# First attention of a two-layer block: block-diagonal queries with full-height score products, and maxima six slots ahead

## The chip, the cores and the metric

The kernel runs on one core of a Trainium2 chip. Its metric is device time in microseconds; the median of three runs before the change is 1698.66 us. The engines named below are TensorE (PE for products, PEld for its weight loads), VectorE (DVE), ScalarE (ACT), GpSimd (POOL) and SyncE (SP), which issues the transfers.

## What is computed

Two layers, each an attention and a feed-forward network with a mixture of experts, over x of 32 batch elements, 128 tokens, 128 features. The change touches the first attention alone, whose 16 heads have 8 features each:

```python
def _L0_xattn_ref(q, k, v, Wq, bq, Wk, bk, Wv, bv, Wo, bo):
    qh = (q @ Wq.T + bq).reshape(B, S, H, Hd).transpose(0, 2, 1, 3)
    kh = (k @ Wk.T + bk).reshape(B, S, H, Hd).transpose(0, 2, 1, 3)
    vh = (v @ Wv.T + bv).reshape(B, S, H, Hd).transpose(0, 2, 1, 3)
    scores = jnp.einsum('bhqd,bhkd->bhqk', qh, kh) / jnp.sqrt(jnp.float32(Hd))
    attn = jax.nn.softmax(scores, axis=-1)
    out = jnp.einsum('bhqk,bhkd->bhqd', attn, vh)
    return out.transpose(0, 2, 1, 3).reshape(B, S, D) @ Wo.T + bo

x = x + _L0_xattn_ref(_layernorm(x), ctx_1024, ctx_1024, ...)   # then ffn 0, attention 1, ffn 1
```

## The kernel before, in words

Blocks follow one another: loads, a small block that rounds a constant `sel0`, the weights of layer 0 (`layer0_weights`), the first attention (`attention0`), its feed-forward network, the second attention, the second network. Each is a block with a barrier at its end, so only `attention0` and what stands ahead of it are touched.

`attention0` works in slots. Slot s is half of the heads of batch element b = s // 2, so there are 64 slots; a group is 4 batch elements, 8 slots. Each engine has one list of instructions, written slot by slot, and waits on semaphores.

- In a slot PE computes the scores of slot s (`scores`), the product of probabilities and values of slot s - 2 (`values`, 24 small products), and the maxima products of slot s + `LM0` (`maxima`). On even slots it also transposes the row maxima (`transpose_maxima`) and projects (`project`); on odd slots it transposes the attention output (`transpose_att`).
- In five of a group's eight slots there is one `fill` as well: transposed x (kind 0), transposed context (1), queries (2), keys (3), values (4) of a later group. All fills and `transpose_maxima` share one PSUM bank, `F_BANK`; each is emptied by ACT (upper half) and DVE (lower half, `lower`) before the next may write it.
- A head's 8 features, split in a high and a low fp16 part, become a contraction of 32 rows (4 combinations of high and low). Queries and keys are written to DRAM (`spill`) and read back four times (`q_x`, `k_x`), so that head 4r + i stands in rows 32i to 32i + 31 of slice r. Products use 32 of the array's 128 rows; two that stand in different row groups are issued side by side. The negated row maxima are added to the scores by a second product with the constant `sel0`.
- ACT takes the exponential of 1024 columns twice per slot (f32 `probs`, fp16 `p_hi`); POOL forms `p_lo` from them; DVE takes the row maxima.
- `transpose_maxima` waits until the last fill has been lowered; `values` of a batch element's first half waits for `s_x`, the residual add (`add`) of the one before, as they share the bank `PV`.

Of the kernel before, what the change touches and what calls it, by code (L numbers as in the profile page):

```python
# [16 lines left out]
P = 128  # L17
# [565 lines left out]
LM0 = 4  # L583
RING0 = 4


def fill_of(s):

    g, at = divmod(s + 11, 8)
    if at < 5 and 0 <= g < G:  # L590
        return g, at
    return None


def fills_before(s):
    return sum(1 for t in range(-11, s) if fill_of(t))


def attention0(nc, mem, psum, x_all, ctx_all, const, w, dram):

    NP = 2 * B
    FIRST, LAST = -11, NP + 4
# [3 lines left out]
    def sb(name, shape, dt=F32):  # L606
        return mem.enter_context(nc.sbuf_tensor(f"{name}_a0", shape, dt))
# [4 lines left out]
    ident, sel = const["ident"], const["sel0"]  # L612
# [6 lines left out]
    q_x, k_x = sb("q_x", [P, 2, 4, 512], F16), sb("k_x", [P, 2, 4, 512], F16)  # L619
    v_hi, v_lo = sb("v_hi", [P, 2, GB, H, D0 + 1], F16), sb("v_lo", [P, 2, GB, H, D0 + 1], F16)  # L620
    negmax, negmax_t = sb("negmax", [P, 2, P]), sb("negmax_t", [P, 2, P], F16)
# [3 lines left out]

    T_BANK, M_BANK, PV, F_BANK = psum[:, 0:4, :], psum[:, 4:6, :], psum[:, 6, :], psum[:, 7, :]
# [4 lines left out]
    s_spill, s_spread = sem("spill"), sem("spread")  # L631
# [4 lines left out]
    with nc.Block() as block:  # L636

        @block.sync
        def _(sp):
            for g in range(G):  # L640
                for m, (hl, wide) in enumerate(((q_hl, q_x), (k_hl, k_x))):
                    sp.wait_ge(s_lo, 5 * g + 3 + m)
                    if g:
                        sp.wait_ge(s_spread, 128 * g)
                    sp.dma_start(dram[m, g % 2], hl[:, :, :]).then_inc(s_spill, 16)
                    sp.wait_ge(s_spill, 32 * g + 16 * m + 16)
                    if g >= 2:
                        sp.wait_ge(s_sc, 8 * (g - 2) + 8)
                    for t in range(4):
                        part = t // 2 if m == 0 else t % 2  # L650
                        src = dram[m, g % 2].rearrange("(r p) l n -> l p r n", p=32)[part]
                        sp.dma_start(wide[t::4, g % 2, :, :], src).then_inc(s_spread, 16)

        @block.tensor
        def _(pe):
            def scores(s):
                b, j = divmod(s, 2)
                tok = slice(b % GB * P, (b % GB + 1) * P)
                par = b // GB % 2
                pe.wait_ge(s_nmt, b + 1)  # L660
                if s >= 2:
                    pe.wait_ge(s_exp_hi, s - 1)
                for r in range(4):
                    for i in (2 * j, 2 * j + 1):
                        rows = slice(32 * i, 32 * i + 32)
                        o = T_BANK[:, 2 * (s % 2) + i % 2, r * P:(r + 1) * P]
                        nc.tensor.matmul(o, k_x[rows, par, r, tok], q_x[rows, par, r, tok], start=True, stop=False)
                    for i in (2 * j, 2 * j + 1):
                        rows = slice(32 * i, 32 * i + 32)
                        o = T_BANK[:, 2 * (s % 2) + i % 2, r * P:(r + 1) * P]  # L670
                        last_ = nc.tensor.matmul(o, sel[rows, r, :], negmax_t[rows, b % 2, :], start=False, stop=True)  # L671
                last_.then_inc(s_sc, 1)

            def maxima(s):
                b, j = divmod(s, 2)
                tok = slice(b % GB * P, (b % GB + 1) * P)
                par = b // GB % 2
                if s % 8 == 0:
                    pe.wait_ge(s_spread, 128 * (s // 8) + 128)
                if s >= 1:  # L680
                    pe.wait_ge(s_max, s)
                for r in range(4):
                    for i in (2 * j, 2 * j + 1):
                        rows = slice(32 * i, 32 * i + 32)
                        last_ = nc.tensor.matmul(M_BANK[:, i % 2, r * P:(r + 1) * P], q_x[rows, par, r, tok],  # L685
                                                 k_x[rows, par, r, tok], start=True, stop=True)
                last_.then_inc(s_mm, 1)

            def transpose_maxima(b, s):
                pe.wait_ge(s_max, 2 * b + 2)  # L690
                if n := fills_before(s):
                    pe.wait_ge(s_lo, n)
                nc.tensor.transpose(F_BANK[:, 0:P], negmax[:, b % 2, :], ident[:]).then_inc(s_nmt_mm, 1)

            def values(s):
                b, j = divmod(s, 2)
                par = b // GB % 2
# [5 lines left out]
                for r in range(4):  # L703
                    for i in (2 * j, 2 * j + 1):
                        h = 4 * r + i
                        o = PV[:, h * (D0 + 1):(h + 1) * (D0 + 1)]
                        q = slice((4 * (i % 2) + r) * P, (4 * (i % 2) + r + 1) * P)
# [64 lines left out]
        def _(act):  # L772
            def fill(s):
# [5 lines left out]
                elif kind < 4:  # L779
                    if g:  # L780
                        act.wait_ge(s_spill, 32 * (g - 1) + 16 * (kind - 1))
                    m = kind - 2
                    nc.scalar.activation((q_hl, k_hl)[m][:, 0, :], F_BANK, ACT.Identity,
                                         bias=w["bias"][:, m:m + 1]).then_inc(s_hi, 1)
                else:
                    if g >= 2:
                        act.wait_ge(s_pv, 8 * (g - 2) + 8)
                    nc.scalar.activation(v_hi[:, g % 2, :, :, 0:D0].rearrange("p j h d -> p (j h) d"),
                                         F_BANK.rearrange("p (h d) -> p h d", d=D0), ACT.Copy).then_inc(s_hi, 1)

            act.wait_ge(s_set, 1)
            for s in range(FIRST, LAST):
# [16 lines left out]
                if even and 0 <= s + LM0 - 2 < NP:  # L809
                    b = (s + LM0 - 2) // 2  # L810
                    act.wait_ge(s_nmt_mm, b + 1)
                    if b >= 2:
                        act.wait_ge(s_sc, 2 * b - 2)
                    nc.scalar.activation(negmax_t[:, b % 2, :], F_BANK[:, 0:P], ACT.Copy, bias=lifted).then_inc(s_nmt, 1)
# [4 lines left out]
        def _(dve):  # L819
# [11 lines left out]
            def lower(s):  # L831
# [11 lines left out]
                else:  # L843
                    last_ = nc.vector.tensor_tensor(
                        v_lo[:, g % 2, :, :, 0:D0].rearrange("p j h d -> p (j h) d"),
                        F_BANK.rearrange("p (h d) -> p h d", d=D0),
                        v_hi[:, g % 2, :, :, 0:D0].rearrange("p j h d -> p (j h) d"), ALU.subtract)
                last_.then_inc(s_lo, 1)

            def maxima(s):  # L850
                b, j = divmod(s, 2)
                dve.wait_ge(s_mm, s + 1)
                if j == 0 and b >= 2:
                    dve.wait_ge(s_nmt_mm, b - 1)
                out = negmax[:, b % 2, 64 * j:64 * j + 64].rearrange("p (i n) -> p i n", n=32)[:, :, 0:4]
                nc.vector.tensor_reduce(out, M_BANK.rearrange("p i (r k) -> p i r k", k=P), AX.X, ALU.max,  # L856
                                        negate=True).then_inc(s_max, 1)
# [17 lines left out]
            nc.vector.memset(negmax[:, :, :], 0.0)  # L875
# [4 lines left out]
            for s in range(FIRST, LAST):  # L880
# [9 lines left out]
                if s % 8 == 2 and (s + 14) // 8 < G:  # L890
                    statistics((s + 14) // 8)

        @block.gpsimd
        def _(pool):
# [14 lines left out]

            normal(0)  # L910
            for s in range(FIRST, LAST):
                if s % 8 == 3 and (s + 13) // 8 < G:
                    normal((s + 13) // 8)
# [448 lines left out]
def program(nc, a, out, spill):  # L1362

    with ExitStack() as mem:
# [18 lines left out]
        def rounded(name, shape, dram, scope):  # L1383

            t = scope.enter_context(nc.sbuf_tensor(name, shape, F16))
            raw_ = scope.enter_context(nc.sbuf_tensor(name + "_raw", shape, F32))
            s1, s2 = (scope.enter_context(nc.semaphore(f"{name}_{i}")) for i in range(2))
            with nc.Block() as block:

                @block.sync  # L1390
                def _(sp):
                    sp.dma_start(raw_[:], dram).then_inc(s1, 16)

                @block.scalar
                def _(act):
                    act.wait_ge(s1, 16)
                    nc.scalar.activation(t[:], raw_[:], ACT.Copy)
            return t

# [29 lines left out]
        with ExitStack() as scope:  # L1429
# [3 lines left out]
            const["sel0"] = rounded("sel0", [P, 4, P], a["c_sel0"], scope)  # L1433
# [86 lines left out]
def constants():  # L1520
# [4 lines left out]
    sel0 = np.zeros((P, 4, P), f)  # L1525
    sel1 = np.zeros((P, 8, P), f)
    for m in range(4):
        sel0[rows % 32 == m, m, :] = 1
# [11 lines left out]
    return {"c_ident": ident, "c_sel0": sel0, "c_sel1": sel1,  # L1540
# [18 lines left out]
```

## Time and profile before

| | us |
|---|---|
| three runs | 1693.28, 1698.66, 1699.65 |
| profiled execution, its time | 1695.49 |
| its span | 1693.7 |
| first to last scores of the first attention | 71.1 to 333.1 |

The profiled execution took 1.8 us more than its span, and lies 3.2 us below the median of the runs. In the rows below, times are microseconds from the span's start; a row of PE is a run of products of one line, and the start of the next row tells when the array took up the next work, since the printed durations of products overlap.

### The profile page before, as it was taken

To read this page: it belongs to the slowest core of one execution; us is meant where nothing else is said; L and a number is where in the kernel's file an instruction comes from. 1 tells how busy PE (TensorE), PEld (TensorE's weight loads), DVE (VectorE), ACT (ScalarE), POOL (GpSimd) and SP (SyncE) were. 2 spreads that over 40 slices of the span, in tenths; PEclk is the share of its full clock that TensorE was granted. 3 is DMA by queue.
4 is the path that set the end of the run, shared out by engine and by line. 5 is a ranking of instruction groups with operands and counts; after the bars stand their busy time and mean duration, and the time that the engine had idled before them with its cause. 6 is when DMAs were issued, how large, how long until landed. Compare 5 with 4: busy or idle time off the path is not lost. (4 is left out here: it accounts for less than half of the span.)

```text
span 1693.7 us, 31779 instructions
## 1 busy us (share of the span) xinstructions
PE 1401.0 (83%) x11720; PEld 1123.0 (66%) x11720; DVE 949.1 (56%) x2066; ACT 814.0 (48%) x1335; POOL 661.4 (39%) x556
## 2 busy tenths in 40 slices
PE   0599999806599999999993798988988989836698
PEld 0477777606488888888882477777777777736486
DVE  0455544337656665666563666665666666527665
ACT  0255655521344444444442465655656556521354
POOL 1266656602155555555552123333232332412254
PEclk9999655555799999999996899998999899965799
DMA  4211111040000000000001000000000000010000
GB/s 114 75 39 39 46 63 45 2 149 1 1 1 1 1 1 1 0 0 0 0 0 62 1 2 1 2 1 3 2 1 3 2 1 2 2 32 1 1 25 25
DMA packets 27575, 31.59 MB, mean 19 GB/s; under 512 B 4721, under 2 KB 21682, under 8 KB 27314
## 3 DMA queue, kind: packets, MB, share of 16 engines
q1 hardware_dynamic: 27442, 29.75, 5.7%
q8 instruction: 91, 1.49, 0.4%
q14 instruction: 42, 0.34, 0.1%
HBM read 23.45 MB, written 6.29 MB: 18 GB/s over the span
## 5 line engine op out<-in xcount | busy, mean ns | idle before, releaser
L1347 POOL TENSOR_TENSOR w_lo_f<-weighted_f,w_hi_f 128x512 fp32r<-128x512 f32 x232 | 300.6, 1296 | 345.8 <-ACT w_hi_f L1289 345.8
L565 POOL TENSOR_TENSOR p_lo_l<-probs_l,p_hi_l 128x512 f16<-128x512 f32 x128 | 148.2, 1158 | 336.5 <-ACT p_hi_l L358 336.5
L1327 DVE TENSOR_TENSOR hidden_f<-psum,gate_act_f 128x512 f32<-128x512 f32 x232 | 160.5, 692 | 210.0 <-PE psum L1239 199.3
L1304 ACT ACTIVATE gate_act_f<-psum 128x512 f32<-128x512 f32 x232 | 138.7, 598 | 269.0 <-PE psum L1239 267.6
L916 POOL TENSOR_TENSOR p_lo_a<-probs_a,p_hi_a 128x1024 f16<-128x1024 f32 x64 | 135.9, 2127 | 112.9 <-ACT p_hi_a L808 112.9
L1333 DVE TENSOR_TENSOR weighted_f<-psum,hidden_f 128x512 f32<-128x512 f32 x232 | 160.5, 692 | 9.0
L1239 PE MATMUL psum<-x_lo_f,w_hi 128*128 (+1 forms) x384 | 153.8, 401 | 0.0
L1237 PE MATMUL psum<-x_hi_f,w_hi 128*128 (+1 forms) x384 | 152.0, 396 | 1.8 <-PEq L1135 1.8
L1238 PE MATMUL psum<-x_hi_f,w_lo 128*128 (+1 forms) x384 | 151.8, 395 | 0.0
L1289 ACT ACTIVATE w_hi_f<-weighted_f 128x512 fp32r<-128x512 f32 x232 | 144.9, 625 | 2.2 <-DVE weighted_f L1333 2.2
L356 ACT ACTIVATE probs_l<-psum,lift_l 128x512 f32<-128x512 f32 x128 | 88.0, 688 | 105.0 <-PE psum L232 105.0
L228 PE MATMUL psum<-q_a_l,k_a_l 64*128 64x128 f16 x512 | 115.9, 226 | 19.2 <-ACT negmax_t_l L350 11.8
L232 PE MATMUL psum<-negmax_t_l,sel 64*128 64x128 f16 x512 | 115.4, 225 | 0.0
L230 PE MATMUL psum<-q_a_l,k_b_l 64*128 64x128 f16 x512 | 115.4, 225 | 0.0
L229 PE MATMUL psum<-q_b_l,k_a_l 64*128 64x128 f16 x512 | 115.4, 225 | 0.0
L856 DVE TENSOR_REDUCE negmax_a<-psum 128x8 f32<-128x1024 f32 x64 | 78.3, 1224 | 42.6 <-PE psum L685 42.6
L807 ACT ACTIVATE probs_a<-psum 128x1024 f32<-128x1024 f32 x64 | 65.5, 1023 | 68.9 <-PE psum L671 68.9
L1243 PE MATMUL psum<-comb_t_f,pick 128*128 (+1 forms) x232 | 92.2, 397 | 0.0
L459 DVE TENSOR_REDUCE negmax_l<-psum 128x4 f32<-128x512 f32 x128 | 87.0, 682 | 1.6 <-PE psum L202 1.3
L358 ACT ACTIVATE p_hi_l<-psum,lift_l 128x512 f16<-128x512 f32 x128 | 87.0, 679 | 0.0
L1237 PEld LDWEIGHTS psum<-x_hi_f,w_hi 128*128 128x128 f32 x384 | 73.3, 191 | 19.1 <-issue 2.2
L1238 PEld LDWEIGHTS psum<-x_hi_f,w_lo 128*128 128x128 f32 x384 | 72.6, 189 | 17.4
(257 smaller groups left out, 3797.9 us busy)
## 6 DMA issues: line engine op xcount, KB each, us to landing
q_x_a<-spill SPq DMA_DIRECT2D x32, 128.0 KB, 2.6
k_x_a<-spill SPq DMA_DIRECT2D x32, 128.0 KB, 2.5
spill<-q_hl_a SPq DMA_DIRECT2D x8, 256.0 KB, 2.0
spill<-k_hl_a SPq DMA_DIRECT2D x8, 256.0 KB, 2.9
out<-x_all SPq DMA_DIRECT2D x8, 256.0 KB, 2.3
pick_raw<-c_pick SPq DMA_DIRECT2D x1, 1536.0 KB, 6.2
stage<-L_ffn_w SPq DMA_DIRECT2D x3, 256.0 KB, 3.0
stage<-L_xattn_Wq SPq DMA_DIRECT2D x1, 512.0 KB, 3.5
```

Source lines behind the costliest of these rows:

```text
L228: nc.tensor.matmul(o, ka, qa, start=True, stop=False)
L229: nc.tensor.matmul(o, ka, q_b[rows, parity, ch, tok], start=False, stop=False)
L565: nc.gpsimd.tensor_tensor(p_lo[:, r, :], probs[:, r, :], p_hi[:, r, :], ALU.subtract).then_inc(s_exp_lo, 1)
L916: nc.gpsimd.tensor_tensor(p_lo[:, s % RING0, :], probs[:, s % 2, :], p_hi[:, s % RING0, :], ALU.subtract).then_inc(s_plo, 1)
L1237: nc.tensor.matmul(dst[:, :], hi[:, a], x1, start=True, stop=False)
L1238: nc.tensor.matmul(dst[:, :], lo[:, a], x1, start=False, stop=False)
L1239: nc.tensor.matmul(dst[:, :], hi[:, a], x2, start=False, stop=True).then_inc(done, 1)
L1289: nc.scalar.activation(w_hi[:, slot, :], weighted[:, (parity * nc_ + k) % 2, :], ACT.Copy).then_inc(s_wh, 1)
L1304: nc.scalar.activation(gate_act[:, slot, :], GATE[slot][:, :], ACT.Silu).then_inc(s_silu, 1)
L1327: nc.vector.tensor_tensor(hidden[:, slot, :], UP[slot][:, :], gate_act[:, slot, :], ALU.mult).then_inc(s_hid, 1)
L1333: nc.vector.tensor_tensor(weighted[:, slot, :], CB[slot][:, :], hidden[:, slot, :], ALU.mult).then_inc(s_a, 1)
L1347: nc.gpsimd.tensor_tensor(w_lo[:, slot, :], weighted[:, (parity * nc_ + k) % 2, :], w_hi[:, slot, :].bitcast(F32), ALU.subtract).then_inc( ...
```

## The change

Queries stand block-diagonally now: `q_pad[:, g, r, i, :]` has head 4r + i in rows 32i to 32i + 31, and zeros in the other 96 rows. One product over all 128 rows with the keys of slice r then gives the scores of four heads, 512 columns. Row 3 of `k_x` holds ones, and the negated maxima of the four heads are written by a transfer into row 3 of `q_pad`, so that the product adds them; `sel0`, its block, its load and its products go. A slot is now slices 2j and 2j + 1 with all four heads, no longer all slices with two heads. The maxima products use `q_pad` as the weights, one head each, all 128 rows.

The zeros are written once per buffer: DVE clears `k_x` (to ones), one group's `q_pad` and a row `nothing`; POOL clears the other two groups' `q_pad`. Queries take 8 transfers per group and one that clears row 3 of the other three heads, keys 4, with the two spills 15; each batch element's maxima take one more. SP's list is now written slot by slot. Three groups' buffers are held, not two. Maxima run 6 slots ahead (`LM0`), not 4; fills stand 3 slots earlier, which swaps the parity of every kind; `statistics` and `normal` of the layer norm move with them.

```diff
-LM0 = 4
+LM0 = 6
...
-    g, at = divmod(s + 11, 8)
+    g, at = divmod(s + FILL0, 8)
...
+            def spread_queries(g):
+                sp.wait_ge(s_spill_q, 16 * g + 16)
+                if g >= NB0:
+                    sp.wait_ge(s_sc, 8 * (g - NB0) + 8)
+                halves = narrow_q[g % 2].rearrange("(r i d) l n -> i (d l) r n", r=4, i=4)
+                for i in range(4):
+                    for t in range(2):
+                        sp.dma_start(q_pad[32 * i + t:32 * i + 32:2, g % NB0, :, i, :], halves[i]).then_inc(s_spread, 16)
...
+            def maxima_row(b):
+                sp.wait_ge(s_nmt, b + 1)
+                tok = slice(b % GB * P, (b % GB + 1) * P)
+                dst = q_pad[3:4, b // GB % NB0, :, :, tok].rearrange("o r i n -> o (r i) n")
+                sp.dma_start(dst, negmax_t[:, b % 4, :]).then_inc(s_row[b % 4], 16)
+
+            sp.wait_ge(s_clear, 3)
+            for s in range(FIRST, LAST):
+                if s % 2 == 0 and 0 <= s + LM0 - 2 < NP:
+                    maxima_row((s + LM0 - 2) // 2)
+                g, at = divmod(s + FILL0, 8)
+                if at == 3 and 0 <= g < G:
+                    spill_queries(g)
+                if at == 4 and 0 <= g < G:
+                    spill_keys(g)
+                if at == 5 and 0 <= g < G:
+                    spread_queries(g)
+                if at == 6 and 0 <= g < G:
+                    spread_keys(g)
...
-                pe.wait_ge(s_nmt, b + 1)
+                pe.wait_ge(s_row[b % 4], 16 * (b // 4 + 1))
                 if s >= 2:
                     pe.wait_ge(s_exp_hi, s - 1)
-                for r in range(4):
-                    for i in (2 * j, 2 * j + 1):
-                        rows = slice(32 * i, 32 * i + 32)
-                        o = T_BANK[:, 2 * (s % 2) + i % 2, r * P:(r + 1) * P]
-                        nc.tensor.matmul(o, k_x[rows, par, r, tok], q_x[rows, par, r, tok], start=True, stop=False)
...
-                        last_ = nc.tensor.matmul(o, sel[rows, r, :], negmax_t[rows, b % 2, :], start=False, stop=True)
+                for r in (2 * j, 2 * j + 1):
+                    last_ = nc.tensor.matmul(T_BANK[:, 2 * (s % 2) + r % 2, :], k_x[:, par, r, tok], q_pad[:, par, r, :, tok],
+                                             start=True, stop=True)
...
-                for r in range(4):
-                    for i in (2 * j, 2 * j + 1):
-                        rows = slice(32 * i, 32 * i + 32)
-                        last_ = nc.tensor.matmul(M_BANK[:, i % 2, r * P:(r + 1) * P], q_x[rows, par, r, tok],
-                                                 k_x[rows, par, r, tok], start=True, stop=True)
+                for r in (2 * j, 2 * j + 1):
+                    for i in range(4):
+                        last_ = nc.tensor.matmul(M_BANK[:, r % 2, i * P:(i + 1) * P], q_pad[:, par, r, i, tok],
+                                                 k_x[:, par, r, tok], start=True, stop=True)
...
-            nc.vector.memset(negmax[:, :, :], 0.0)
+            nc.vector.memset(nothing[:, :], 0.0)
+            nc.vector.memset(k_x[:, :, :, :], 1.0)
+            nc.vector.memset(q_pad[:, 0, :, :, :], 0.0).then_inc(s_clear, 1)
...
+            nc.gpsimd.memset(q_pad[:, 1, :, :, :], 0.0).then_inc(s_clear, 1)
+            nc.gpsimd.memset(q_pad[:, 2, :, :, :], 0.0).then_inc(s_clear, 1)
             normal(0)
...
-            const["sel0"] = rounded("sel0", [P, 4, P], a["c_sel0"], scope)
```

On PE an even slot of before, here the one with the keys' fill, issues its scores as four pairs of two query products and two `sel` products, then the transposed maxima, then eight maxima products:

```order
L667 MATMUL psum<-q_x_a,k_x_a 128x128 x2
L671 MATMUL psum<-negmax_t_a,sel 128x128 x2
...
L693 MATMUL psum<-ident,negmax_a 128x128
L685 MATMUL psum<-k_x_a,q_x_a 128x128 x8
L740 MATMUL psum<-c_hi_a,wk_hi 128x512
L741 MATMUL psum<-c_lo_a,wk_hi 128x512
L742 MATMUL psum<-c_hi_a,wk_lo 128x512
```

After the change the keys' fill stands in an odd slot, ahead of the transposed attention output, and the even slot that follows carries the values' fill:

```order
L777 MATMUL psum<-c_lo_a,wk_hi 128x512
L778 MATMUL psum<-c_hi_a,wk_lo 128x512
L752 MATMUL psum<-ident,att_a 128x128
L705 MATMUL psum<-q_pad_a,k_x_a 128x512 x2
L729 MATMUL psum<-ident,negmax_a 16x128
L719 MATMUL psum<-k_x_a,q_pad_a 128x128 x8
L756 MATMUL psum<-wo,att_t_a 128x128
L757 MATMUL psum<-bo,ones 128x128
L783 MATMUL psum<-wv_hi,c_hi_a 128x128
```

Sixteen score products became two of 512 columns; the eight maxima products are eight still, but each takes the whole array.

On SP the list of one group before is a spill and four reads for the queries, then the same for the keys, and then the next group's:

```order
L645 DMA spill<-q_hl_a 128x1024
L652 DMA q_x_a<-spill 32x4x512 x4
L645 DMA spill<-k_hl_a 128x1024
L652 DMA k_x_a<-spill 32x4x512 x4
L645 DMA spill<-q_hl_a 128x1024
```

After, the same group's list has the maxima rows of the group being computed (`q_pad_a<-negmax_t_a`) between its transfers:

```order
L651 DMA narrow_q<-q_hl_a 128x1024
L679 DMA q_pad_a<-negmax_t_a 1x16x128
L655 DMA narrow_k<-k_hl_a 128x1024
L664 DMA q_pad_a<-narrow_q 16x4x512 x8
L666 DMA q_pad_a<-nothing_a 1x4x1536
L679 DMA q_pad_a<-negmax_t_a 1x16x128
L673 DMA k_x_a<-narrow_k 32x4x512 x3
L673 DMA k_x_a<-narrow_k 31x4x512
```

The keys' four transfers now stand behind the wait for one of those rows' maxima.

On DVE the first attention begins before with three small clears ahead of the statistics:

```order
L875 MEMSET negmax_a 128x256
L876 MEMSET v_lo_a 128x128
L877 MEMSET v_hi_a 128x128
L822 BN_STATS stats_a<-x_all 128x6 x4
L828 BN_AGGR meanvar_a<-stats_a 128x2 x4
```

After, there are five, and two of them are large; the fp16 zeros are cleared as half as many 4-byte words:

```order
L912 MEMSET nothing_a 1x768
L913 MEMSET k_x_a 128x6144
L914 MEMSET q_pad_a 128x4096
L915 MEMSET v_lo_a 128x192
L916 MEMSET v_hi_a 128x192
L860 BN_STATS stats_a<-x_all 128x6 x4
L866 BN_AGGR meanvar_a<-stats_a 128x2 x4
```

POOL now begins with two clears, where before its first work was the layer norm of group 0:

```order
L949 MEMSET q_pad_a 128x8192
L950 MEMSET q_pad_a 128x8192
L936 ISA
L936 TENSOR_TENSOR vareps_a<-meanvar_a,eps 128x4
L939 TENSOR_TENSOR rstd_a<-vareps_a,power 128x4
L945 TENSOR_SCALAR xhat_a<-x_all,meanvar_a,rstd_a 128x128 x4
```

Everything that the block computes waits for that first layer norm, so the clears moved ahead of it.

## Rows read from the trace of the kernel before

**Rows 1.** Busy time of each engine in two stretches, granted clock, transfers.

```profile
100.00:120.00 20.00, 18.74 (x238) 14.67 (x232) 10.24 (x22) 10.40 (x15) 8.71 (x6) 1.00 0.25 81
240.00:260.00 20.00, 18.60 (x251) 14.01 (x248) 11.38 (x24) 12.05 (x19) 11.83 (x9) 0.59 0.23 80
```

**Rows 2.** Groups of instructions by form, 72 to 335 us.

```profile
L916 POOL TENSOR_TENSOR p_lo_a<-probs_a,p_hi_a 128x1024 f16<-128x1024 f32 x63 | 133.8, 2127 | 111.7 <-ACT p_hi_a L808 111.6
L807 ACT ACTIVATE probs_a<-psum 128x1024 f32<-128x1024 f32 x64 | 65.5, 1023 | 68.9 <-PE psum L671 68.9
L814 ACT ACTIVATE negmax_t_a<-psum 128x128 f16<-128x128 f32 x31 | 8.8, 285 | 0.0
L906 POOL TENSOR_SCALAR xhat_a<-x_all,meanvar_a,rstd_a 128x128 f32<-128x128 f32 x24 | 18.7, 793 | 0.6
L693 PE MATMUL psum<-ident,negmax_a 128*128 128x128 f32 x31 | 14.1, 456 | 7.9 <-DVE q_hl_a L841 3.5 <-DVE v_lo_a L844 2.4 <-DVE x_lo_a L837 2.0
```

**Rows 3.** Timeline of PE in slots with no fill, at 122 us.

```profile
122.05 0.28 PE L667 MATMUL psum<-q_x_a,k_x_a 32*128 32x128 f16 x2
...
123.01 0.47 PE L693 MATMUL psum<-ident,negmax_a 128*128 128x128 f32 x1
123.42 0.61 PE L685 MATMUL psum<-k_x_a,q_x_a 32*128 32x128 f16 x8
123.95 0.80 PE L720 MATMUL psum<-wo,att_t_a 128*128 128x128 f32 x2
...
125.65 0.17 PE L709 MATMUL psum<-v_hi_a,p_hi_a 128*128 128x9 f16 x1 [0.48 <-DVE x_all L873]
...
126.37 0.29 PE L667 MATMUL psum<-q_x_a,k_x_a 32*128 32x128 f16 x2
```

**Rows 4.** Timeline of PE around the keys' and the values' fill, at 107 us.

```profile
107.09 0.77 PE L740 MATMUL psum<-c_hi_a,wk_hi 128*128 128x512 f32 x1
...
108.51 0.23 PE L709 MATMUL psum<-v_hi_a,p_hi_a 128*128 128x9 f16 x1
...
111.53 0.47 PE L747 MATMUL psum<-wv_hi,c_hi_a 128*128 128x128 f32 x1
...
114.15 0.43 PE L716 MATMUL psum<-ident,att_a 128*128 128x128 f32 x1
```

**Rows 5.** The score products of L667: durations least, median, most (ns).

```profile
L667 PE MATMUL psum<-q_x_a,k_x_a x512: 214/309/310, 71.1 to 333.0; 32*128 32x128 f16 x171
```

**Rows 6.** Timeline of PE four groups later, at 245 us.

```profile
245.67 0.77 PE L740 MATMUL psum<-c_hi_a,wk_hi 128*128 128x512 f32 x1
...
247.84 0.23 PE L667 MATMUL psum<-q_x_a,k_x_a 32*128 32x128 f16 x2
...
248.39 0.18 PE L709 MATMUL psum<-v_hi_a,p_hi_a 128*128 128x9 f16 x1
```

**Rows 7.** Timeline of all engines from 20 to 61 us.

```profile
20.80 0.36 SPq L1392 DMA_DIRECT2D sel_raw<-c_sel  x1
...
24.25 0.35 SPq L972 DMA_DIRECT2D raw_wq<-L_xattn_Wq  x1
...
33.08 0.27 DVE L875 MEMSET negmax_a<- 128x256 f32 x1 [0.39 <-PEq L967]
...
37.27 3.13 POOL L906 TENSOR_SCALAR xhat_a<-x_all,meanvar_a,rstd_a 128x128 f32<-128x128 f32 x4
40.46 0.72 PEld L736 LDWEIGHTS psum<-ident,xhat_a 128*128 128x128 f32 x4 [8.59 <-POOL xhat_a L906]
...
56.45 2.52 SPq L652 DMA_DIRECT2D k_x_a<-spill  x4
...
60.99 0.29 PE L685 MATMUL psum<-k_x_a,q_x_a 32*128 32x128 f16 x2 [6.15 <-DMA k_x_a<-spill]
```

**Rows 8.** A large and a small clear elsewhere in the program.

```profile
L1150 DVE MEMSET comb_t_f<- 32x4096 f32 x5 | 17.4, 3472 | 4.5 <-issue 4.5
0.24 0.10 POOL L1550 MEMSET const-float32-0.0<- 128x1 f32 x1 [0.24 <-issue]
```

More of the change, by code:

```diff
@@ L595, in fills_before @@
 def fills_before(s):
-    return sum(1 for t in range(-11, s) if fill_of(t))
+    return sum(1 for t in range(-FILL0, s) if fill_of(t))
 def attention0(nc, mem, psum, x_all, ctx_all, const, w, dram):
     NP = 2 * B
-    FIRST, LAST = -11, NP + 4
+    FIRST, LAST = -FILL0, NP + 4
     scale = float(np.float32(1.0) / np.sqrt(np.float32(D0)))
@@ L610, in sem @@
         return mem.enter_context(nc.semaphore(f"{name}_a0"))
-    ident, sel = const["ident"], const["sel0"]
+    ident = const["ident"]
     xhat = sb("xhat", [P, GB, D])
@@ L630, in attention0 @@
     s_fill, s_hi, s_lo = sem("fill"), sem("hi"), sem("lo")
-    s_spill, s_spread = sem("spill"), sem("spread")
+    s_spill_q, s_spill_k, s_spread = sem("spill_q"), sem("spill_k"), sem("spread")
+    s_row = [sem(f"row_{n}") for n in range(4)]
+    s_clear = sem("clear")
     s_mm, s_max, s_nmt_mm, s_nmt = sem("max_mm"), sem("max"), sem("nmt_mm"), sem("nmt")
@@ L639, in _, with spill_queries @@
         def _(sp):
[L640 to L652, printed above, removed]
+            def spill_queries(g):
+                sp.wait_ge(s_lo, 5 * g + 3)
+                if g >= 2:
+                    sp.wait_ge(s_spread, SPREADS * 16 * (g - 1))
+                sp.dma_start(narrow_q[g % 2], q_hl[:, :, :]).then_inc(s_spill_q, 16)
@@ new lines, in spread_keys @@
+            def spread_keys(g):
+                sp.wait_ge(s_spill_k, 16 * g + 16)
+                halves = narrow_k[g % 2].rearrange("(r p) l n -> l p r n", p=32)
+                for t in range(4):
+                    skip = int(t == 3)
+                    sp.dma_start(k_x[t + 4 * skip::4, g % NB0, :, :], halves[t % 2, skip:32]).then_inc(s_spread, 16)
+            def maxima_row(b):
[3 more added lines that the diff above has]
+                sp.dma_start(dst, negmax_t[:, b % 4, :]).then_inc(s_row[b % 4], 16)
@@ L811, in _ @@
                     act.wait_ge(s_nmt_mm, b + 1)
-                    if b >= 2:
-                        act.wait_ge(s_sc, 2 * b - 2)
-                    nc.scalar.activation(negmax_t[:, b % 2, :], F_BANK[:, 0:P], ACT.Copy, bias=lifted).then_inc(s_nmt, 1)
+                    if b >= 4:
+                        act.wait_ge(s_row[b % 4], 16 * (b // 4))
+                    nc.scalar.activation(negmax_t[:, b % 4, :], F_BANK[0:H, 0:P], ACT.Copy, bias=lifted).then_inc(s_nmt, 1)
                 if fill_of(s):
@@ L889, in _ @@
                     lower(s)
-                if s % 8 == 2 and (s + 14) // 8 < G:
-                    statistics((s + 14) // 8)
+                if s % 8 == 7 and (s + 17) // 8 < G:
+                    statistics((s + 17) // 8)
         @block.gpsimd
@@ L1381, in program @@
         const["s_power"] = mem.enter_context(nc.semaphore("power_set"))
[L1383 to L1398, printed above, removed]
         maskt = sb("mask_rows", [B, P])
@@ L1539, in constants @@
             pick1[h * 16 + e, n // P, n % P] = 1
-    return {"c_ident": ident, "c_sel0": sel0, "c_sel1": sel1,
+    return {"c_ident": ident, "c_sel1": sel1,
             "c_pick0": pick0, "c_pick1": pick1,
```

68 lines of the change are left out of this document (38 added, 30 removed).

## The prediction, made before the changed kernel was run

> **What bounds the kernel now.** I first read the busy time in stretches, to see which engine the first attention waits for. In two stretches of 20 us PE is busy 18.7 and 18.6 us, while DVE, ACT and POOL stand at 8.7 to 12.4 [rows 1]. The groups of instructions say the same from the other side: POOL waits 111.7 us for ACT's exponentials, and ACT 68.9 us for scores [rows 2]. So PE's own list sets the pace, and I price the change on it from the starts of runs of products.
>
> A slot's eight maxima products, issued two by two, take 123.42 to 123.95, 0.53 us; its sixteen score products take 122.05 to 123.01, 0.96 us [rows 3]. Four more pairs cost 0.43 us: a pair costs 0.107 us, and each run 0.10 us besides, which I read as the array emptying where 32-row and full-height products meet. Values take 0.72 us (125.65 to 126.37) [rows 3]. The keys' fill, three products of 512 columns, takes 1.42 us and the values' fill 2.62 us [rows 4]. The keys' fill of a group four groups later starts at 245.67, against 107.09 here [rows 4, 6]: 138.6 us, 34.7 us per group of eight slots.
>
> These paces are those of the lower level of the array's clock, 1.2 GHz (128 columns in 0.107 us). Score products last 309 ns at the median and 214 at the least [rows 5], so nearly all of the block runs at the lower level. The stretch at 100 us is labelled with a granted clock of 1.00, but its products go at the lower pace; only from its first recorded change does the label mean something, as the 0.59 of the stretch at 240 us [rows 1]. There the clock rose for a few microseconds, and a slot's scores took 0.55 us (247.84 to 248.39) [rows 6]. What PE did just before was the projection and the keys' fill, its most unbroken full-height work.
>
> **The change on PE, at the lower clock, per group.** Scores: 1024 columns as before, 0.86 us a slot. Maxima: eight products one after the other, 8 x 0.107 = 0.86 where four pairs took 0.43, so 8 x 0.43 = +3.4 us. Both kinds, the values and the small transposes are now all full-height, so the 0.10 us at each meeting goes: eight in two slots, 32 in a group, -3.2 us. No row shows fp16 full-height score products, so the bounds are no saving (+3.4 net) and all of it (+0.2); I take +0.2, since scores are now the same two long streams as two thirds of the keys' fill, which shows 0.43 us for each 512 columns.
> The fills swap parity. The wait of the values for the residual add is 0.8 us (the projection's run is 1.70 us, 123.95 to 125.65 [rows 3], while its four products at the pace of the values' fill, twelve in 2.62 us [rows 4], would be 0.9), and a fill between hides it: it falls in one even slot of four instead of two, -0.8 us. The transposed maxima wait for the last fill's lowering after three kinds of fill now, 7.9 us in all [rows 2], and after two kinds then: -0.2 us. The longer maxima also cover the attention output's division ahead of its transpose, -0.2 us.
> What is late next: SP issues the keys' four transfers behind the wait for the maxima of the slot's batch element. Those come about 3.3 us into slot 8g - 8 (scores 0.87, two exponentials of 1.02, a copy of 0.29 [rows 2]); four issues are 2.5 us and the landing as long again (56.45 to 60.99, 4.5 us for both) [rows 7], so the keys stand at 3.3 + 0.4 + 4.6 = 8.3 to 8.7 us. The maxima of the new group stand two slots and a run of scores later on PE: 4.3 (an even slot with no fill, its runs as priced above and the 0.8 us wait) + 2.7 (an odd one) + 1.1 = 8.1 us. That is 0.6 us of wait for PE per group, with the projection, the fill and the values queued behind it. The maxima rows' own transfers have four slots, some 16 us, and are hidden; if SP were held up that long, PE would wait for them instead. The other transfers of a group are hidden too: queries are issued a slot earlier, and bytes are about as before.
> Sum per full group: +0.2 - 0.8 - 0.2 - 0.2 + 0.6 = -0.4 us. With six such groups and two without fills (+0.3 each), the steady part is -2 us.
>
> A rule speaks against this change. The Trainium skill (TensorE: Matmul & The Clock Gate, Part 3: Packing small matmuls) would place small contractions in distinct row groups so that they run at the same time. The pairs at 0.107 us for two agree. By that rule alone the maxima lose and nothing comes back: +27 us for 64 slots. The Trainium skill (TensorEngine Tiling, Key Properties) also says that a change of tiling mode drains the engine; by that, the 0.10 us goes and the sum stays near zero.
>
> **Startup.** The block with `sel0` goes: 20.80 to 24.25, -3.4 us [rows 7]. DVE clears 768 + 6144 + 4096 elements before its statistics. A clear of 4096 took 3.47 us [rows 8], 0.85 ns each, so 9.3 us; with it the statistics end 9 us later. POOL clears twice 8192 before the first layer norm. Its only clear in the trace is of one element (0.10 us) [rows 8]. From below it is free, and DVE's 9 us decide; from above it costs what POOL's subtraction does, 2127 ns per 1024 [rows 2], 17 us each, 31 us of delay. I take DVE's rate, since a clear reads nothing: 7 us each. Work that was to start at 35.9 then starts at 47.1, +11.2 us; nothing hides it, as PE waits for that layer norm from its first fill on [rows 7]. Nine transfers in place of four ahead of the keys': +1.5. Two more slots ahead of the first scores, minus the fills and maxima taken out of the steady part: +1. Startup: -3.4 + 11.2 + 1.5 + 1 = +10.3, from +8 to +30.
>
> **The clock.** At the lower level the sum is +8. But scores, maxima, projection and fills now follow each other as unbroken full-height products, such as stood before the rise at 247 us, and in every slot rather than once a group. I expect the clock to rise often. At the upper level a slot's scores cost 0.45 and its maxima 0.45 us (8 x 0.055 [rows 6]), fills and projection half, the values' 0.7 us stay. PE's sum falls to 19 us a group, and POOL with 8 x 2.127 + 4 x 0.793 and the small steps, 21.4 us [rows 2], and ACT with 16 x 1.02 and its copies, 21.7, are the floor. For the handshakes on `F_BANK` I add 3 us by choice: 25, and the keys' wait grows to 2.2 us, as slots are shorter and SP's transfers are not: 27 us. The idle time so made should send the clock down again, so I take half of the time at each level: 1 / (0.5/27 + 0.5/34.3) = 30.2 us, -4.5 x 6 groups = -27 us, and -3.8 for each of the two groups without fills, -7.6. Half of the time is a choice; no row fixes it.
>
> Sum: 1695.5 (profiled) + 10.3 - 27 - 7.6 = 1671. The median of the runs lies 3 us above the profiled time, so I forecast 1672 to be compared with 1698.7.
>
> **Rivals.**
> 1. The clock stays up nearly throughout. For it: no idle stretch of PE is long. Against: POOL and ACT become the bound, and PE idles a quarter. 27 us a group: 1695.5 + 10.3 - 46 - 14 = 1646. Chance 0.17; half or thereabouts 0.47.
> 2. The clock stays down, and the full-height products bring neither gain nor loss. For it: 309 ns at nearly all score products now, though PE is busy 93%. 1695.5 + 10.3 - 2 = 1704. Chance 0.16.
> 3. Slower: the 0.10 us at each meeting is not a matter of height but of every run's end, and stays, at the lower clock. Then the maxima's +0.43 us a slot is paid in full: 1704 + 26 less hidden waits = 1727. It decides if a slot's maxima take 0.96 us rather than 0.86. Chance 0.10.
> 4. POOL's clears cost 17 us each: +20 on any case; with half of the clock it gives 1692, with the low clock 1724. Chance 0.10.
>
> **Numbers.** The measurement tells from no change only what exceeds 0.5%, 8.5 us. Faster: case 1, the forecast (0.64 together) and a little of 4: 0.66. Same: case 2 mostly: 0.14. Slower: 3, most of 4, part of 2: 0.20. The range runs from 1640 (clock up, quick clears) to 1712 (low clock with a few us more at the start). The likeliest case's own range is 1655 to 1690.
>
> **What would show it.** First transposed x near 48 instead of 40.5 us; eight maxima products at 0.107 us pitch where the clock is low, with no 0.10 us before the next run; durations of score products in two clusters, and a granted clock between 0.6 and 0.9 in the block; a wait of PE for the keys' transfer once per group; the block from first to last scores in 227 us instead of 262. The prediction is wrong if the clock does not move, if POOL's clears are slow, or if PE waits for a maxima row in each batch element.

## The result

| | before | after |
|---|---|---|
| median (lowest to highest) of four runs, us | 1697.94 (1693.28 to 1699.65) | 1720.74 (1715.38 to 1722.39) |
| profiled execution, its time / its span | 1695.49 / 1693.7 | 1715.38 / 1713.5 |
| first maxima products | 61.0 | 77.3 |
| first to last scores | 71.1 to 333.1 | 95.2 to 353.3 |
| last scores to end of span | 1360.6 | 1360.2 |

The change makes the kernel slower: ratio 1.0133 [1.0103, 1.0164]. The forecast was 1672 with a range up to 1712: the change went the other way, and the time lies outside that range. Everything behind the first attention is as it was. The loss lies ahead of the first scores (24 us), and the block itself gives back 4 us where the forecast had 35.

**The clock did rise.** First the products themselves in the trace of after (durations least/median/most, first and last start), and two stretches of 20 us with the columns of [rows 1].

```profile
L705 PE MATMUL psum<-q_pad_a,k_x_a x128: 376/379/634, 95.2 to 353.3; 128*128 128x512 f16 x128
L719 PE MATMUL psum<-k_x_a,q_pad_a x512: 216/219/330, 77.3 to 338.9; 128*128 128x128 f16 x171
...
120.00:140.00 20.00, 14.43 (x207) 10.39 (x203) 11.22 (x24) 12.86 (x20) 14.60 (x12) 0.83 0.24 77
240.00:260.00 20.00, 11.65 (x161) 9.22 (x162) 9.09 (x14) 11.30 (x17) 10.63 (x6) 0.83 0.06 21
```

The median product of 128 columns is now a quick one (219 ns; it was 309 in [rows 5]), and the granted clock reads 0.83 where it read 0.59 [rows 1]. Yet PE is busy 14.4 and 11.7 us of 20, where it was busy 18.6. Part of that is the quicker pace; the rest is idle time. The timeline of PE shows for what (start, busy, run; in brackets the idle time ahead and its releaser).

```profile
129.39 0.59 PE L705 MATMUL psum<-q_pad_a,k_x_a 128*128 128x512 f16 x2
...
137.41 0.38 PE L729 MATMUL psum<-ident,negmax_a 128*16 128x128 f32 x1 [0.18 <-DVE negmax_a L893]
143.76 1.03 PE L719 MATMUL psum<-k_x_a,q_pad_a 128*128 128x128 f16 x8 [5.97 <-DMA k_x_a<-narrow_k]
144.59 0.74 PE L756 MATMUL psum<-wo,att_t_a 128*128 128x128 f32 x2
...
163.32 0.59 PE L705 MATMUL psum<-q_pad_a,k_x_a 128*128 128x512 f16 x2
...
166.87 0.17 PE L745 MATMUL psum<-v_hi_a,p_hi_a 128*128 128x9 f16 x1 [1.37 <-DVE x_all L910]
171.32 0.28 PE L729 MATMUL psum<-ident,negmax_a 128*16 128x128 f32 x1 [0.38 <-DVE negmax_a L893]
...
177.64 1.03 PE L719 MATMUL psum<-k_x_a,q_pad_a 128*128 128x128 f16 x8 [6.04 <-DMA k_x_a<-narrow_k]
```

Once per group the first maxima products wait 6 us for the keys. From 143.76 to 177.64 a group takes 33.9 us, where the prediction read 34.7 from one stretch of four groups [rows 4, 6]; over the first six groups the mean is 34.1 both before and after (the table under "All of it together"). The waits between the first and the last scores, summed (us, times, longest):

```profile
PE psum L719 <- DMA k_x_a<-narrow_k: 44.9, 7, 7.5
PE psum L745 <- DVE x_all L910: 13.8, 14, 1.4
```

What the transfer does in that time is seen at its first occurrence, in stretches of 1 us (the last three numbers are granted clock, busy share of the 16 DMA engines, GB/s).

```profile
70.00:71.00 1.00, 0.00 (x0) 0.00 (x0) 0.00 (x0) 0.00 (x0) 0.52 (x1) 1.00 0.20 57
71.00:72.00 1.00, 0.00 (x0) 0.00 (x0) 0.00 (x0) 0.00 (x0) 0.00 (x0) 1.00 0.06 9
...
73.00:74.00 1.00, 0.00 (x0) 0.00 (x0) 0.00 (x0) 0.00 (x0) 0.00 (x0) 1.00 0.07 24
...
76.00:77.00 1.00, 0.00 (x0) 0.00 (x0) 0.00 (x0) 0.00 (x0) 0.00 (x0) 1.00 0.06 23
```

From 71 to 77 us nothing computes, and the share is 0.06 to 0.07: one engine of 16 is 0.0625. One engine moves 24 GB/s, and the only transfer that fits is the keys' fourth, of 31 rows (row 3 of `k_x` holds the ones and is skipped): 124 KB at 24 GB/s is 5.3 us. The Trainium skill (DMA: Bandwidth & Descriptors, Why a DMA increments its semaphore by 16 and not by 1) says that a transfer is dealt to the largest number of engines, up to 16, that divides the slowest dimension of both of its sides, here the 31 rows. 31 is a prime, so the number is 1; the trace agrees, with a share of 0.06.

The start of the trace of after, which answers to [rows 7]:

```profile
29.65 6.92 POOL L949 MEMSET q_pad_a<- 128x8192 f16 x1 [29.22 <-POOLq L1008]
31.80 5.18 DVE L913 MEMSET k_x_a<- 128x6144 f16 x1 [1.23 <-issue]
37.78 3.47 DVE L914 MEMSET q_pad_a<- 128x4096 uint32 x1 [0.80 <-issue]
...
48.95 1.12 PE L772 MATMUL psum<-ident,xhat_a 128*128 128x128 f32 x4 [19.87 <-POOL xhat_a L945]
60.83 5.15 SPq L664 DMA_DIRECT2D q_pad_a<-narrow_q  x8
66.03 0.71 SPq L666 DMA_DIRECT2D q_pad_a<-nothing_a  x1
66.78 2.69 SPq L673 DMA_DIRECT2D k_x_a<-narrow_k  x4
```

### The profile page after: what moved, and what is told of

It is laid out like the page before. It is cut to its first block and busy times, and to the rows that moved or that the text cites. A ratio compares the mean times of both kernels' runs of the same rounds, so it can differ in the third digit from the quotient of the medians.

```text
span 1713.5 us, 30032 instructions
## 1 busy us (share of the span) xinstructions
PE 1339.2 (78%) x10824; PEld 1072.2 (63%) x10824; DVE 956.7 (56%) x2068; ACT 808.5 (47%) x1334; POOL 675.8 (39%) x558
## 5 line engine op out<-in xcount | busy, mean ns | idle before, releaser
L893 DVE TENSOR_REDUCE negmax_a<-psum 128x8 f32<-128x1024 f32 x64 | 78.0, 1219 | 88.6 <-PE psum L719 88.5
L719 PE MATMUL psum<-k_x_a,q_pad_a 128*128 128x128 f16 x512 | 49.5, 254 | 59.8 <-DMA k_x_a<-narrow_k 58.9
```

## The experiments

Theory A: the transfer of 31 rows runs on one DMA engine, and costs 5 us at the start and 4 to 5 us in each group. Theory B: SP issues the keys late, behind the wait for a maxima row, as the forecast had it. Theory C: the queue is slow because some 13 transfers stand ahead of the keys. Theory D: the shape of the products (full height, and so no longer two side by side), and no other part of the change, raises the clock. Where an expectation weighs another cause, it names it there. Ratios are to the kernel before, run on the same chip. The edits of the keys' transfers are shown without their semaphore increments.

### 31 rows cut into 16 and 15

```diff
-for t in range(4):
-    skip = int(t == 3)
-    sp.dma_start(k_x[t + 4 * skip::4, g % NB0, :, :], halves[t % 2, skip:32])
+for t in range(3):
+    sp.dma_start(k_x[t::4, g % NB0, :, :], halves[t % 2])
+sp.dma_start(k_x[7:68:4, g % NB0, :, :], halves[1, 1:17])
+sp.dma_start(k_x[71::4, g % NB0, :, :], halves[1, 17:32])
```

> The keys' transfer of 31 rows is cut into one of 16 rows and one of 15. Theory A (one engine of 16 carries the whole 31-row transfer, 124 KB at some 24 GB/s): the stretch of about 6 us in which the DMA share is 0.06 goes, PE's wait of 6.0 us per group for the keys falls below 1.5 us, first maxima products 5 to 6 us earlier, time about 44 us lower, near 1677 us. Theory B (the keys are late because they are issued behind the wait for a maxima row): no change, 1720. Theory C (the queue is slow because some 13 transfers stand ahead of the keys): no change, or a few us more for the added transfer.

Measured: 1685.43 us, ratio 0.9938 [0.992, 0.9957]. First the 1 us stretches at its start, then two waits of the block, two starts of PE and the score products (busy us, mean ns).

```profile
70.00:71.00 1.00, 0.00 (x0) 0.00 (x0) 0.00 (x0) 0.00 (x0) 0.75 (x1) 1.00 0.60 180
71.00:72.00 1.00, 0.00 (x0) 0.00 (x0) 0.00 (x0) 0.00 (x0) 0.00 (x0) 1.00 0.20 62
72.00:73.00 1.00, 0.81 (x8) 0.81 (x9) 0.00 (x0) 0.00 (x0) 0.00 (x0) 1.00 0.00 0
...
PE psum L720 <- DMA k_x_a<-narrow_k: 14.5, 7, 2.6
PE psum L746 <- DVE x_all L911: 12.5, 14, 1.4
...
129.25 0.62 PE L720 MATMUL psum<-k_x_a,q_pad_a 128*128 128x128 f16 x8 [2.17 <-DMA k_x_a<-narrow_k]
159.17 1.03 PE L720 MATMUL psum<-k_x_a,q_pad_a 128*128 128x128 f16 x8 [2.10 <-DMA k_x_a<-narrow_k]
...
L706 PE MATMUL psum<-q_pad_a,k_x_a 128*128 128x512 f16 x128 | 50.2, 483 | 0.0
```

The six microseconds of one engine are gone, the first maxima stand at 72.2 instead of 77.3, and these two starts lie 29.9 us apart (over six groups the mean is 30.7). One transfer more, of the same bytes, takes 35 us off the median and turns the sign of the change. Theory A holds, though the time is 8 us above what it expected; B and C forecast no change here. What follows varies the number of rows on the one engine.

### The keys' issues ahead of the maxima row in SP's list

```diff
 for s in range(FIRST, LAST):
+    g, at = divmod(s + FILL0, 8)
+    if at == 6 and 0 <= g < G:
+        spread_keys(g)
     if s % 2 == 0 and 0 <= s + LM0 - 2 < NP:
         maxima_row((s + LM0 - 2) // 2)
```

> SP issues the four key transfers of slot 8g - 8 ahead of that slot's maxima row instead of behind it. Theory A (one engine carries 31 rows): only the row's own 0.6 us of issue is won, some 5 us in all, about 1716. Theory B (the wait for the maxima row ahead of them makes them late): the 6 us per group go almost wholly, about 1677. Theory C (transfers ahead in the queue): as A.

Measured: 1716.04 us, ratio 1.0121 [1.009, 1.0151]; the wait for the keys is 43.3 us in 7 times, where it was 44.9. Its SP and that of after, in the same group (start, time to issue):

```profile
131.61 0.69 SPq L666 DMA_DIRECT2D q_pad_a<-nothing_a  x1
132.34 2.64 SPq L673 DMA_DIRECT2D k_x_a<-narrow_k  x4
```

```profile
125.81 0.58 SPq L655 DMA_DIRECT2D narrow_k<-k_hl_a  x1
126.44 5.60 SPq L664 DMA_DIRECT2D q_pad_a<-narrow_q  x8
132.08 0.68 SPq L666 DMA_DIRECT2D q_pad_a<-nothing_a  x1
132.81 0.58 SPq L679 DMA_DIRECT2D q_pad_a<-negmax_t_a  x1
133.44 2.69 SPq L673 DMA_DIRECT2D k_x_a<-narrow_k  x4
```

Theory B falls. In both lists the issues follow each other with no gap: the row costs its own issue of 0.6 us and no wait. What stands ahead of the keys' issues is the nine of the queries, 126.44 to 132.76; a list with the keys ahead of the queries was not run.

### 31 rows cut into 17 and 14, and 32 rows throughout

As 16 + 15, with the two last transfers so:

```diff
+sp.dma_start(k_x[7:72:4, g % NB0, :, :], halves[1, 1:18])
+sp.dma_start(k_x[75::4, g % NB0, :, :], halves[1, 18:32])
```

> The keys' transfer of 31 rows is cut into 17 and 14 rows. Theory A, if a number of rows without a small divisor is what puts a transfer on one engine: 17 rows are on one engine still, 68 KB instead of 124, so the one-engine tail shrinks from about 6 to about 3 us and the wait per group with it; time about halfway, 1697 to 1703. If any cut helps, by the number of transfers alone: as e1_split, 1677. Theories B and C: 1720.

Measured: 1703.89 us, ratio 1.0039 [1.0027, 1.0051].

```profile
71.00:72.00 1.00, 0.00 (x0) 0.00 (x0) 0.00 (x0) 0.00 (x0) 0.00 (x0) 1.00 0.20 65
72.00:73.00 1.00, 0.00 (x0) 0.00 (x0) 0.00 (x0) 0.00 (x0) 0.00 (x0) 1.00 0.07 24
...
PE psum L720 <- DMA k_x_a<-narrow_k: 33.4, 7, 5.5
```

The same number of transfers as 16 + 15 and the same bytes, but the share falls to 0.07 and 24 GB/s again, for two microseconds instead of six. The time is 1 us above the 1697 to 1703 that was expected.

```diff
+for t in range(4):
+    sp.dma_start(k_x[t::4, g % NB0, :, :], halves[t % 2])
```

> All four key transfers carry 32 rows, so that row 3 of k_x no longer holds ones but keys; the scores get another number in place of the maxima (the only part changed). 15 transfers per group as in the changed kernel. Theory A: as e1_split or a little better, 1675 to 1680, since no transfer has 31 rows. Theories B and C: 1720.

This one overwrites the row of ones, so that the scores get another number in place of their maxima. Measured: 1686.74 us, ratio 0.994 [0.9924, 0.9957], 10.3 us of waits for the keys in 7. So the sum of these waits goes 44.9, 33.4, 14.5, 10.3 us for rows on one engine of 31, 17, none and none. With 32 rows a group has as many transfers as after, so theory C falls too.

### Only the shapes of the products, in the kernel before

```diff
-# scores: 8 products of 32 rows with k_x, q_x, and 8 with sel, negmax_t
+for r in (2 * j, 2 * j + 1):
+    nc.tensor.matmul(T_BANK[:, 2 * (s % 2) + r % 2, :], k_x[:, par, r, tok], q_x[:, par, :, tok], start=True, stop=True)
-# maxima: 8 products of 32 rows
+for r in range(4):
+    for i in (2 * j, 2 * j + 1):
+        nc.tensor.matmul(M_BANK[:, i % 2, r * P:(r + 1) * P], q_x[:, par, i, tok], k_x[:, par, r, tok], start=True, stop=True)
```

The products taken out are told in two comments. Everything else is the kernel before: its transfers, clears, two groups, four slots ahead. The numbers are not the attention's: heads are summed, the maxima are not added (the exponential's scale is divided by 1000 to keep it finite).

> The kernel before with the shapes of the products alone changed: a slot's scores as two full-height products of 512 columns, its maxima as eight full-height products of 128. Transfers, clears, fills and slots are those of before; the numbers are not attention scores (heads are summed, the maxima are not added, the exponential's scale is divided by 1000). Theory D (full-height products raise the clock): score products near 380 ns at the median, granted clock 0.7 to 0.9 in the block, a group of eight slots 29 to 31 us instead of 34.7, time 1665 to 1675. Theory E (the clock rises because of the new order of fills or the waits): granted clock near 0.5 to 0.55, group 34 to 35.5 us, time 1695 to 1705.

Measured: 1656.57 us, ratio 0.9778 [0.9749, 0.9807]. Its score products, their mean (busy us, mean ns), and 200 to 240 us of the kernel before and of this one:

```profile
L664 PE MATMUL psum<-q_x_a,k_x_a x128: 376/379/634, 71.1 to 293.2; 128*128 128x512 f16 x128
...
L664 PE MATMUL psum<-q_x_a,k_x_a 128*128 128x512 f16 x128 | 48.7, 470 | 0.0
...
200.00:240.00 40.00, 37.80 (x515) 30.00 (x514) 19.57 (x36) 22.70 (x34) 23.39 (x15) 0.50 0.13 41
200.00:240.00 40.00, 32.43 (x435) 24.04 (x436) 23.52 (x42) 27.71 (x42) 32.16 (x22) 0.87 0.13 41
```

Theory D holds: at equal clock the maxima take the array twice as long, and yet the block falls from 262 to 222 us, with a granted clock of 0.87 where it was 0.50. Each half of it alone:

> As the run before it in this list, but only the scores have the full-height shape; the maxima stay 32-row pairs (the maxima are not added and the exponential's scale is divided by 1000). Theory D: the clock rises part of the time, granted 0.6 to 0.8, time 1670 to 1690. Theory E: granted clock near 0.5, each slot some 0.1 to 0.2 us shorter by the meetings of heights saved, 1685 to 1695.

Measured: 1678.2 us (1669.43 to 1696.7, a wide spread), ratio 0.9893 [0.9869, 0.9917]; first to last scores 239.0 us.

> As the first in this list, but only the maxima have the full-height shape; the scores stay 32-row pairs with the second product (the maxima are those of summed heads, the exponential's scale is divided by 1000). Theory D: the clock rises part of the time, which pays for the doubled maxima: 1680 to 1700. Theory E: the maxima's 0.43 us a slot comes on top, less 0.1 us for a meeting of heights: 1712 to 1720.

Measured: 1676.61 us, ratio 0.9882 [0.9862, 0.9903]; first to last scores 240.7 us. The profiled execution is the slowest of its five, and what it loses lies behind the last scores (1379 us instead of 1361). The two traces, 200 to 240 us, scores only and then maxima only:

```profile
200.00:240.00 40.00, 34.72 (x414) 23.97 (x413) 22.92 (x42) 25.61 (x39) 26.31 (x17) 0.70 0.21 69
```

```profile
200.00:240.00 40.00, 33.72 (x597) 29.00 (x596) 23.39 (x50) 25.73 (x38) 26.97 (x19) 0.83 0.24 74
```

Each takes 21 to 23 us off the block, both together 40. In maxima only, the maxima take the array twice as long at equal clock, and the kernel is 20 us quicker, where theory E (the order of fills or the waits raises the clock) expected it 15 to 20 us slower. Not separated is what about the shape counts: a full-height product also has the array to itself, where two of 32 rows ran side by side, and the scores became fewer and longer. That the numbers in the array differ in these three kernels is not the cause, since the clock rises in after too, where they are the right ones.

### The clears behind the first layer norm

On top of 16 + 15: DVE clears behind `statistics(0)`, POOL behind `normal(0)`; the ones go to POOL, and SP waits for the other two groups' zeros only when it needs them.

```diff
+nc.gpsimd.memset(k_x[:, :, :, :], 1.0).then_inc(s_clear, 1)      # behind normal(0)
+nc.gpsimd.memset(q_pad[:, 1, :, :, :], 0.0).then_inc(s_later, 1)
+nc.gpsimd.memset(q_pad[:, 2, :, :, :], 0.0).then_inc(s_later, 1)
```

> The split key transfers, and the clears moved behind the first layer norm: on DVE behind the first statistics, on POOL behind the first normalisation, with the ones of k_x on POOL too. If the clears set the start, first transposed x at about 38 us instead of 49, and the whole time 9 to 11 us below the run with the split alone (1685): 1675. If something else would hold the start, less than 3 us.

Measured: 1676.74 us, ratio 0.9898 [0.9866, 0.993].

```profile
37.80 1.11 PE L775 MATMUL psum<-ident,xhat_a 128*128 128x128 f32 x4 [8.37 <-POOL xhat_a L947]
60.83 1.03 PE L722 MATMUL psum<-k_x_a,q_pad_a 128*128 128x128 f16 x8 [8.66 <-DMA k_x_a<-narrow_k]
```

The first transposed x and the first maxima come 11.4 us earlier than in 16 + 15 (49.20 and 72.2); the whole gains 9.

### The residual add and the projection ahead of the maxima

In even slots, on PE and on DVE, once on 16 + 15 and once on the kernel before:

```diff
+if even and 0 <= s - 4 < NP:
+    project((s - 4) // 2)      # and add(...) on DVE
 if 0 <= s + LM0 < NP:
     maxima(s + LM0)
-if even and 0 <= s - 4 < NP:
-    project((s - 4) // 2)
```

> The split key transfers, and in even slots PE projects ahead of the maxima products, DVE adds ahead of its row maxima. Theory F (at the upper clock the values wait for DVE's add, which stands behind 1.22 us of row maxima: 1.37 us in each even slot that has no fill): that wait goes, about 12 us over the block, time near 1673. Rival (POOL and ACT already set the pace there, or the row maxima come later and hold up the next slot's products by as much): within 3 us of the run with the split alone, 1685.

Measured: 1679.47 us, ratio 0.9886 [0.9867, 0.9906]. It gains 6 us on 16 + 15, half of what was expected: the wait for the add fell, and the one for the keys grew.

```profile
PE psum L720 <- DMA k_x_a<-narrow_k: 23.0, 7, 3.9
PE psum L746 <- DVE x_all L911: 3.4, 9, 0.5
```

> The kernel before with the projection and the add first in even slots. Its wait for the add is 0.48 us printed, 8.6 us in 18 waits, at the lower clock. Theory F: up to 9 us less, 1688 to 1692. Rival: the wait moves to the maxima or to the transposed maxima, 1695 to 1700.

Measured: 1692.12 us, ratio 0.9967 [0.9954, 0.998]; the block takes 257.5 us, 4.4 less than before, where up to 9 were expected.

### All of it together

16 + 15, the keys' issues first, the clears behind, the projection first:

> Split key transfers, keys issued ahead of the maxima row, clears behind the first layer norm, projection and add first. If the parts add up: 1685 - 9 (clears) - 12 (add) - 4 (order of issue) = 1660. If the add's wait only moves: 1672.

Measured: 1667.87 us, ratio 0.982 [0.9803, 0.9837]. First maxima stand at 60.6, scores from 76.6 to 303.0 (226.4 us), and 16.9 us of waits for the keys in 7 are left. It is faster than both kernels, but 8 us short of the 1660 of parts that add up.

The starts of the scores show where in the block each run gains. Fills stand in the first 48 slots, six groups; behind them before has two more (keys' and values', slots 48 and 49), after and its variants none.

| run | first scores | scores of slot 48 | last scores | a group, mean of the first six | last 16 slots |
|---|---|---|---|---|---|
| before | 71.1 | 275.6 | 333.1 | 34.1 | 57.5 |
| before, projection first | 71.2 | 275.5 | 328.7 | 34.1 | 53.2 |
| before, shapes alone | 71.1 | 242.6 | 293.2 | 28.6 | 50.6 |
| after | 95.2 | 299.9 | 353.3 | 34.1 | 53.4 |
| 16 + 15 | 88.0 | 272.1 | 321.2 | 30.7 | 49.1 |
| 32 rows throughout | 89.1 | 274.2 | 323.6 | 30.8 | 49.4 |
| 16 + 15, clears behind | 78.7 | 262.8 | 313.1 | 30.7 | 50.3 |
| 16 + 15, projection first | 89.1 | 272.8 | 316.3 | 30.6 | 43.5 |
| all of it | 76.6 | 261.0 | 303.0 | 30.7 | 42.0 |

The scores of slot 48 in before, after, 16 + 15 and 16 + 15 with the projection first:

```profile
275.64 0.29 PE L667 MATMUL psum<-q_x_a,k_x_a 32*128 32x128 f16 x2
...
299.92 0.59 PE L705 MATMUL psum<-q_pad_a,k_x_a 128*128 128x512 f16 x2
...
272.14 0.59 PE L706 MATMUL psum<-q_pad_a,k_x_a 128*128 128x512 f16 x2
...
272.75 0.59 PE L706 MATMUL psum<-q_pad_a,k_x_a 128*128 128x512 f16 x2
```

Projection first gains nothing in the groups with fills, on either kernel; nearly all of its gain lies in the last 16 slots. And the five variants of after in which no transfer of the keys is on one engine take 30.6 to 30.8 us a group, whether PE waits 10.3, 14.5 or 23.0 us in all for the keys. What holds a group at that time no run shows.

## Why the prediction was wrong

**The step that failed** is the keys' wait: "four issues are 2.5 us and the landing as long again", priced at 0.6 to 2.2 us a group. The 4.5 us came from the four reads of 32 rows in [rows 7]; the landing of 31 rows takes 5 us more. The other times of the step came out near: in slot 8g - 8, which starts at 129.39, the keys' first issue stands at 133.44, 4.1 us in (forecast 3.7), and PE is ready for the new maxima 5.97 us ahead of 143.76, 8.4 us in (forecast 8.1, at the lower clock). The first of these is luck: SP issues without a gap from 125.81 on, so the queries' nine issues set it, not the wait for the maxima. But from the first issue to the landing are 10.3 us, priced at 4.6. The list of SP had `k_x_a<-narrow_k 31x4x512` as a row of its own, and the forecast gave it the price of its neighbours. With the rows dealt as 16 and 15 the wait is 14.5 us over 7 (2.1 each), within what was priced, though not for the reason given: the wait for the maxima row is not it (keys' issues first gives 43.3 for 44.9). 16 + 15 recovers 5.1 us up to the first maxima, 2.1 from there to the first scores and 24.9 in the block, 32 us of the 44 by which the profiled time misses its forecast (1715.4 against 1671); of these 2.5 are lost again behind the last scores. The other 12 are two terms of the forecast: the first scores come 16.9 us later than before instead of 10.3, and the block gains 28.8 us instead of 34.6.

**The clock, right in kind, but priced a third too high.** Full-height products raise it, shown by the shapes alone in the old order (-40 us). The group with fills was priced at 30.2 us and takes 30.7 without the slow transfer. It was to fall from 34.7, but that figure is one stretch of four groups and the mean of six was 34.1, so they gain 20.4 us (204.5 to 184.1) instead of 27. In after they gain nothing: the wait for the keys takes all of it. The half at each level was a choice; the mean score product of 16 + 15, 483 ns between 379 and 634, says that six in ten were quick. By the label, 0.83 in two stretches of after would be two thirds at the upper level (0.83 = 0.67 x 1 + 0.33 x 0.5), but 0.74 and 0.66 in the same stretches of 16 + 15 are a half and a third. Rival 1 (27 us a group) did not come: even the shapes alone leave 222 us for the block, where it would have 202. The packing that the prediction weighed against the change works (two 32-row products take 0.107 us), but its +27 us did not come: maxima alone at full height take 20 us off.

**The groups without fills, -7.6 us forecast: the number came, in part by luck.** The last 16 slots take 49.1 us with 16 + 15 and took 57.5, 8.4 less (in after 4.1 less). But 4.0 us of it are the two fills that stood there before (1.42 and 2.62 us at the lower clock [rows 4]) and now stand ahead of the first scores, with two slots' maxima; so it is work moved as much as a quicker pace. Part of what held these groups is the add: projection first, which shortens that wait, takes 5.6 us more off them with 16 + 15 and 4.3 on the kernel before.

**The 0.10 us at each meeting: right.** At the lower clock eight maxima take 143.76 to 144.59, 0.83 us for 8 x 0.107 = 0.86, with nothing over before the next run. So rival 3, which asked for 0.96, falls.

**Startup, right up to the first transposed x** (48.95, forecast 48; POOL's clears 6.92 us, forecast 7, so rival 4 falls). Two terms were small: nine transfers in place of four take 60.83 to 66.74 to issue, 5.9 us for 2.5, so +3.4 instead of +1.5; and first maxima to first scores is 15.8 us in 16 + 15, and was 10.1, so +5.7 instead of +1; two more slots and two more fills stand there. That the clears were on the path is shown: moved, they give 9 us back.

**The add's wait.** Priced at -0.8 a group for its parity at the low clock; the add is waited for 13.8 us over 14, 1.4 us at most, where the printed wait was 0.48 [rows 3]. In the groups with fills this cost nothing: with projection first the wait falls from 12.5 to 3.4 us, and they take 30.6 us as with 16 + 15 alone.

**One reading of the rows** was off without effect: DVE, ACT and POOL stand at 8.7 to 12.05 us in [rows 1], not to 12.4.

What the rest of the change costs can be read against the shapes alone, by their spans: 1654.6 to 1683.9 with 16 + 15. Of these 29 us, 11 lie ahead of the first maxima (60.9 to 72.2), 6 between these and the first scores (10.2 to 15.8), 11 in the block (222.1 to 233.2), 1 behind it. The shapes alone leave out the maxima's addition and the block-diagonal zeros, so this is a comparison, not a goal. All of the 11 us in the block lie in the six groups with fills (184.1 against 171.5; the last 16 slots are 1.5 quicker), and since the group's time does not follow the keys' wait, it stays open what they are.

## What to carry to other kernels

Read the row count of every transfer against the number of DMA engines: one that was left with 31 or 17 rows ran on one engine at 24 GB/s here, and cutting it in 16 and 15 costs one issue. An array's clock can be worth more than its packing: products of 32 rows side by side do the same columns in half the time at equal clock (0.53 us against 0.83), and left the clock at its lower level here. When an engine's clock doubles, price the waits of the slots again at the new pace, since the transfers and DVE don't speed up with it (a row maximum on DVE took 1224 ns before and 1219 with 16 + 15). And look in which groups a run gains: a wait can shrink, as the add's did, in groups that something else holds.

## What the runs showed of the hardware

- 31 rows of 4 KB landed at 24 GB/s with a DMA share of 0.06 to 0.07, 17 rows the same, while with 16 and 15 rows all of the keys' transfers were through by 72 us, at 180 GB/s from 70 to 71.
- From 200 to 240 us the granted clock was 0.50 before, 0.70 with full-height scores alone, 0.83 with full-height maxima alone and 0.87 with both. The block's gain did not follow the label (23, 21 and 40 us).
- Clears cost 0.85 ns an element on both engines by their printed durations: POOL 8192 in 6.92 us, DVE 6144 in 5.18 and 4096 words of 4 bytes in 3.47. POOL's second clear starts 6.9 us behind the first; DVE's second large one starts 5.98 us behind the first (31.80 to 37.78), so there 0.97 ns an element.
- SP issued its transfers without a gap at 0.6 to 0.7 us each: eight in 5.15 to 5.60 us, four in 2.69.
